# A two-layer graph attention kernel: GpSimd makes one of eight sign tiles in every second chunk of layer 0

## What is computed

```python
# layer 0 (layer 1 has the same form, with W transposed)
h = jnp.maximum(_layernorm(x, axis=-1), 0.0)
Wh = h @ W
e = leaky_relu((Wh @ a1)[:, None] + (Wh @ a2)[None, :], 0.2)
scores = jnp.where(adj > 0, e, -9e15)
attention = jax.nn.softmax(scores, axis=1)
x = x + jax.nn.elu(attention @ Wh)
```

## Time and profile before

| | us |
|---|---|
| median of 3 runs | 1372.12 |
| lowest and highest | 1363.56, 1382.64 |
| the profiled execution | 1364.02 |
| its span in the trace | 1362.3 |
| busy over the span: PE, DVE, ACT, POOL | 1148.8, 1216.7, 1190.0, 313.3 |
| start of the layer 0 groups, end of the loads, end of layer 0's groups | about 103, 708, 779 |

### The profile page before, as it was taken

The page is one execution under the profiler, slowest core; times in us unless marked ns, Lnnn a source line. Parts: engine busy times, 40 slices in busy tenths (PEclk is TensorE's granted clock), DMA queues, the critical chain, the costliest instruction groups (busy, mean ns, idle before and its releaser), DMA issues.

```text
span 1362.3 us, 52779 instructions
## 1 busy us (share of the span) xinstructions
PE 1148.8 (84%) x20826; PEld 1118.0 (82%) x20826; DVE 1216.7 (89%) x2191; ACT 1190.0 (87%) x1825; POOL 313.3 (23%) x520
## 2 busy tenths in 40 slices
PE   2727988989888898998988762999899989999997
PEld 2527988988888898898988751999899989989997
DVE  6688889998899898999897869989999989998997
ACT  2338999999999999999999736999999989998995
POOL 2443544444444444444430000000000000000000
PEclk9858999999999998999999976999999999998999
DMA  8999999999999999999993010000101010010001
GB/s 157 172 204 199 212 191 200 211 211 212 210 199 212 211 211 212 208 212 211 211 176 56 9 29 25 2 26 2 34 2 33 2 34 10 25 33 2 18 2 25
DMA packets 128148, 157.08 MB, mean 115 GB/s; under 512 B 59296, under 2 KB 59424, under 8 KB 128032
## 3 DMA queue, kind: packets, MB, share of 16 engines
q0 software_dynamic: 73728, 134.25, 53.3%
q1 hardware_dynamic: 54304, 21.11, 7.1%
HBM read 285.25 MB, written 4.26 MB: 213 GB/s over the span
## 4 chain that ended last, share of the span: by engine, by line
PE 32%; issue 21%; DVE 18%; ACT 12%; DMA 9%; DVEq 1%; ACTq 1%; POOLq 0%; POOL 0%; SPq 0%
PE psum L1367 30%; ACT toggle L607 9%; DMA stream<-in_adj_dram 7%; DVE work L1003 5%; DVE work L1039 3%; DVE toggle L1034 3%; DVE stream L773 2%; ACT stream L624 2%; PE psum L1261 2%; DVE toggle L1016 1%; DMA x_scratch<-y_tile 1%; DVE work L871 1%; PE psum L1348 1%; ACT sums L624 0%; DMA s_row<-s_scratch 0%
## 5 line engine op out<-in xcount | busy, mean ns | idle before, releaser
L1367 PE MATMUL psum<-parts_d,toggle 128*128 128x130 f16 x8192 | 979.9, 222 | 43.6 <-DVE work L1039 42.1
L1367 PE MATMUL psum<-parts_g,work 128*128 128x130 f16 x8192 | 979.8, 222 | 0.0
L1367 PEld LDWEIGHTS psum<-parts_d,toggle 128*128 128x128 fp8e4 x8192 | 802.9, 98 | 48.8 <-issue 48.4
L1367 PEld LDWEIGHTS psum<-parts_g,work 128*128 128x128 fp8e4 x8192 | 809.5, 99 | 5.2 <-issue 1.7
L607 ACT ACTIVATE toggle<-s_row,steep_d 128x512 uint8 (+1 forms) x952 | 591.0, 729 | 0.9
L607 ACT ACTIVATE toggle<-stream,steep_d 128x1024 uint8<-128x1024 f32 x419 | 443.4, 1155 | 27.5 <-PE psum L1367 27.5
L708 POOL DMA_DIRECT2D stream<-in_adj_dram x512 | 312.0, 611 | 371.0 <-DVE stream L773 308.6
L1034 DVE TENSOR_TENSOR toggle<-work,toggle 128x1024 int32<-128x1024 int32 x256 | 312.1, 1219 | 69.1 <-ACT toggle L607 66.3
L1039 DVE TENSOR_TENSOR work<-work,toggle 128x1024 int32<-128x1024 int32 x256 | 311.4, 1216 | 0.8
L773 DVE TENSOR_SCALAR stream<-stream 128x1024 bf16<-128x1024 bf16 x512 | 200.3, 419 | 33.0 <-DMA stream<-in_adj_dram 28.1
L1261 PE MATMUL psum<-pack_w,stream 128*128 128x8 bf16 x4096 | 132.4, 166 | 66.0 <-DVE stream L773 56.6
(11 more groups left out here) (135 smaller groups left out, 362.1 us busy)
## 6 DMA issues: line engine op xcount, KB each, us to landing
stream<-in_adj_dram POOLq DMA_DIRECT2D x512, 256.0 KB, 7.6
s_row<-s_scratch SPq DMA_DIRECT2D x16, 256.0 KB, 6.0
stream<-s_scratch SPq DMA_DIRECT2D x8, 512.0 KB, 3.9
toggle<-in_x_dram SPq DMA_DIRECT2D x4, 512.0 KB, 6.8
x_tile<-in_x_dram SPq DMA_DIRECT2D x16, 128.0 KB, 10.6
x_scratch<-y_tile SPq DMA_DIRECT2D x16, 128.0 KB, 9.5
stream<-x_scratch SPq DMA_DIRECT2D x4, 512.0 KB, 5.3
stream<-x_scratch SPq DMA_DIRECT2D x8, 256.0 KB, 4.2
```

The costliest lines, as they stand in the source:

```text
L1367: ins = nc.tensor.matmul(psum[:, bank, COLS[third]:COLS[third + 1]], mask.bitcast(FP8), parts[e][:, t, :, :].rearrange("p k h -> p (k h)") ...
```

## The change

POOL makes the last of the eight sign tiles in the even chunks of layer 0, in all 16 groups (64 tiles). DVE keeps its one in the odd chunks and no longer makes one in the even chunks of the last two groups. ACT makes seven in every chunk of layer 0. POOL's tile stands in its queue between the fourth and the fifth load of a row tile; for the last two groups it stands behind all loads. Ahead of it POOL waits for the ring (`chunk_used`) and the row (`row_in`); DVE waits for it ahead of L1034 (`signs_pool`). Row tiles 4 to 6 are now loaded by an unrolled loop, the 56 from 7 on by a loop of seven rounds with eight in each.

```diff
+    SIGN_FROM = 7
...
-        return int(c % 2 == 1 or (isinstance(g, int) and g >= GROUPS - 2))
+        return c % 2
+
+    def pool_tiles(L, c):
+
+        return int(L == 0 and c % 2 == 0)
...
-                for j in range(CTS[L] - own_tiles(L, g, c)):
+                for j in range(CTS[L] - own_tiles(L, g, c) - pool_tiles(L, c)):
...
+            def pool_sign(g, side, c):
+
+                pool.wait_ge(chunk_used, chunk(0, g, c) + 1)
+                pool.wait_ge(row_in, (g + 1) * 16)
+                t = (c + 1) * CTS[0] - 1
+                settled(pool)
+                nc.gpsimd.tensor_scalar(tog[0][:, c % TOG, CTS[0] - 1, :], s_row0[:, side, :], minus_d[:, t:t + 1], float(MARK),
+                                        ALU.is_gt, ALU.mult).then_inc(signs_pool, 1)
...
-            with pool.Fori(GT, TILES) as r:
+            for r in range(GT, SIGN_FROM):
                 load_adj(r, r * STEPS)
+            with pool.Fori(0, GROUPS // 2 - 1) as h:
+                for p in range(2 * GT):
+                    row_tile = h * (2 * GT) + (SIGN_FROM + p)
+                    first_step = h * (2 * GT * STEPS) + (SIGN_FROM + p) * STEPS
+                    load_adj(row_tile, first_step, range(0, STEPS // 2))
+                    pool_sign(h * 2 + p // GT, p // GT, 2 * (p % GT))
+                    load_adj(row_tile, first_step, range(STEPS // 2, STEPS))
+            load_adj(TILES - 1, (TILES - 1) * STEPS)
+            for g in range(GROUPS - 2, GROUPS):
+                for j in range(GT):
+                    pool_sign(g, g % 2, 2 * j)
             reduce_tops(1)
...
                 between(0)
+                if pool_tiles(L, c):
+                    dve.wait_ge(signs_pool, g * (CHUNKS[0] // 2) + (c // 2 + 1))
                 dve.wait_ge(sign_ready, n + 1)
```

More of the change, by code:

```diff
@@ L115, in own_up_to @@
         usual = sum(own_tiles(0, 0, k) for k in range(CHUNKS[0]))
[L116 to L125, removed]
+        if L == 0:
+            return g * usual + here
+        start = LGROUPS[0] * usual
+        if isinstance(g, int) and g == 0:
+            return start + here
+        first, each = [sum(own_tiles(1, h, k) for k in range(CHUNKS[1])) for h in range(2)]
+        return (g - 1) * each + (start + first + here)
     def chunk(L, g, c):
@@ L317, in gat2_kernel @@
         signs_dve = sem("signs_dve")
+        signs_pool = sem("signs_pool")
         chunk_used = sem("chunk_used")
```

## The result

| | before | after |
|---|---|---|
| median, us | 1377.38 (4 runs, 1363.56 to 1385.35) | 1415.75 (4 runs, 1415.05 to 1423.42) |
| the profiled execution's span | 1362.3 | 1414.2 |
| last load issued | 700.5 | 747.1 |
| from there to the end | 661.8 | 667.1 |

The ratio after to before is 1.0313, with a 95% interval of 1.0256 to 1.0369: slower by 3.1%. The forecast was 1378, the range ended at 1405.

The account below looks back on a forecast made before the run. Load transfers at 209 GB/s, 42.5 us a group, were taken as the bound. From 1364.02: load stretch 0, exclusion +7, group 14 +1, end -2 gave 1370, carried over to the median as 1378; range 1356 to 1405.

Parts of the forecast that it names:

- The bound: Load stretch, 190 to 700 us: transfers at 209 GB/s, 42.5 us a group, set the pace; ACT's relief is worth 0.
- ACT the bound: Rival, load stretch: ACT sets the pace and transfers follow, 34 us won there and 2 at the end, 1336; chance 0.06.
- The price of the sign: POOL's TENSOR_SCALAR, four a group: 0.82 us each from the AFFINE_SELECT row, plus 0.2 for the hand-over.
- The exclusion: Groups 0 to 13: POOL's sign and DVE's work exclude each other, putting 4.1 us a group on DVE; +7 us over 14.
- the other side: Rival that POOL gets in only when DVE stands still, deciding from 1.4 us a sign: 1415, chance 0.22.
- With 7.6 us of landing time in hand this is covered.: Loads queued behind the sign on POOL: the fifth is about 1 us late, covered by landing time; cost 0.
- The wait of POOL for its inputs, "0": Ahead of the sign on POOL's queue: chunk_used and row_in are both met long before, so waiting costs 0.
- Group 14, +1: First sign of group 14 stands behind tile 63's eight loads and DVE's unpacks may hold it off: 1 us, once.
- the end, -2: After the loads, ACT enters the last two groups earlier, so DVE waits less for it: 2 us gained, between 0 and 10.
- POOL is locked out until DVE stands still: Rival, load stretch: signs run only at DVE's wait, DVE pays 17 us and dry DMA 28; 1415, chance 0.22.

Follow-up runs that it names:

- tile_left_out: Kernel after, with the eighth sign tile of layer 0's even chunks made by nobody and DVE's wait for it gone: 1367.0 us, ratio 0.996.
- forms: Kernel before, with single POOL operations (memset, signs of several widths, addition, cast) at its very start, each awaited: sign of 512 columns 2.0 us; no kernel time given.
- last_two_groups: Kernel after, with POOL making only the eight signs of groups 14 and 15, behind all loads, and none between loads: 1386.8 us, ratio 1.011.

## Why the prediction was wrong, point by point

- **The bound.** Right. 209 or 210 GB/s with a full and with a lighter ACT (tile_left_out), and ACT's relief worth about nothing. "ACT the bound" (1336) is out.
- **The price of the sign.** Mis-sized: 0.82 us from the AFFINE_SELECT, 2.0 us alone (forms). 1.4 us had been named as the point from which the other side decides.
- **The exclusion.** The mechanism was right, the loser wrong. The sum charged DVE with 4 x 1.02 us a group. DVE pays 0.4 us a sign (454.12 us in 11.2 groups of 45.4 are 40.4 a group, against 38.9); POOL pays, 3.4 us a sign instead of 2.0. DVE's back to back operations held POOL off in three signs of four, two-input masks as well as converts and unpacks, up to 9.94 us for a quarter sign.
- **"With 7.6 us of landing time in hand this is covered."** The step that failed. It was reasoned for a fifth load late by 1 us and priced at 0. At 3.4 us, four times a group, the period goes from 42.5 to (42.5 + 2.9) us: 41 of the 52 us between the two spans, some 7 of which the spread of executions may hold. The 7.6 us were not in hand. What covers a stand is the loads under way when it begins, 1.3 us each, less the time that the next load takes at least: at 549.27 that is 5.1 less 3.8, so 1.3 us for a sign of 4.28. The other four of the eight slots held loads that had landed and waited for their converts.
- **The wait of POOL for its inputs, "0".** Right for `chunk_used` and `row_in`; but the first sign has a pause of 9.4 us that no semaphore explains, 5.4 us of the loss. The 7.1 <-issue of the earlier trace rows stood in the profile of before and was read past.
- **Group 14, +1, and the end, -2.** From the last load's issue to the first mask of group 14 after had 4.0 us (747.1 to 751.12), before 2.6: +1.4, right. The gain of 2 didn't come; from the last load to the end it is 5.3 longer, of which 1.4 is this and the rest isn't assigned. DVE's waits for ACT behind the loads are as before, 11.4 us against 10.7.
- **The rival "POOL is locked out until DVE stands still", 1415, chance 0.22.** What happened, and by its numbers nearly: a sign above 1.4 us, a rate under 200, waits for loads and for POOL's tile. But not as it was split. It put 17 us on DVE and 28 on the dry DMA; measured are 41 in the stream, 5 at the first sign, and a DVE that waits more and is busy less than before. It also reckoned with a landing of 2 us or more; the shortest in the stretch is 3.8. That its total of 1415 meets the 1415.75 is luck, since two of its terms are wrong and offset each other. Its chance was too low, because the price of the sign was set by the one small operation that the trace had, while the two ends stood at 0.82 and 2.89 us.

## What to carry to other kernels

A queue that issues the transfers which bound the kernel is itself on the critical path: work between two issues costs what the transfers in flight don't cover, here 0.7 to 1.3 us for 3 to 4, though every engine has idle time. On POOL, don't price an operation by its elements alone while VectorE runs back to back: one that reads can last until VectorE pauses (here three of four were held off), and one that only writes holds VectorE's converts up instead. And look for MODIFY_POOL_CONFIG with idle time behind it in the profile you have: here the pause came again when POOL went from the reduction to another kind of operation, though not for memsets.

## What the runs showed of the hardware

- A compare-and-multiply TENSOR_SCALAR on POOL, 128x512 f32 to uint8, takes 2.0 us; a comparison or addition alone 1.57; a cast 0.79; a memset 0.52.
- POOL's operations that read SBUF were held off by VectorE, so that a sign of 128 columns took up to 9.9 us, 0.7 alone. Where one got in first, VectorE was held up instead (a sum 1.18 us in place of 0.69). Memsets of 128x1200 were hardly stretched (1.12 and 1.18 us) and made VectorE's converts 0.51 and 0.63 us in mean instead of 0.42, and left its masks at 1.21 to 1.22.
- A pause of 7 to 12 us stands before POOL's AFFINE_SELECT, the first PARTITION_ALL_REDUCE and the first TENSOR_SCALAR after it, each with two MODIFY_POOL_CONFIG at its start; none before memsets or a TENSOR_SCALAR right behind the AFFINE_SELECT.
- In some executions TensorE's queue stands for 7.0 to 7.7 us, with 9 more packets on the instruction queue for each time: the page of the profile has 94 such packets in the kernels with none, 103 with one (last_two_groups), 112 with two, 121 with three. At one such place, 450 to 455 us of last_two_groups, PE does nothing. The waits and the window there:

```profile
PEld psum L1284 <- issue: 7.5, 1, 7.5
...
450.00:455.00 5.00, 0.00 (x0) 0.00 (x0) 3.07 (x5) 5.00 (x14) 1.69 (x4) 0.86 1.11 222
```

  Up to there that execution issues its loads 2 us earlier than before's, from 513 us on 8 to 9 us later, and the last one 7.6 later. The packets on the instruction queue fall into such a stand (in the stretch of the loads before has none), so it looks like a second fetch of instructions that were held already; what brings it on is open. It comes up to three times in seven of the kernels with added work on POOL, last_two_groups among them, whose added work stands behind all loads, and not at all in the profiled executions of before and after, so it is no part of the loss explained here, but a part of that of the kernels with a number in the last column.
